# Cross attention in a two-layer kernel: value products split over the column halves of the PE array, softmax sums as separate 32-column products

## The reference, cut to what matters

```
q, k   = rmsnorm(per head) of layernorm(x) @ Wq.T, and of the two key projections
p      = exp(q @ k.T / 8 - max)                       # 1024 x 1101 per head and batch
o      = (p @ v) / sum(p)
x      = x + concat(o over heads) @ Wo.T + bo
```

## Time and profile before

| | before |
|---|---|
| median of 3 runs | 1112.41 us (1111.99 to 1117.14) |
| the profiled execution: its time | 1111.86 us |
| its span, from the first to the last instruction | 1110.1 us |
| TensorE busy in matmuls | 976.9 us, 88% |
| VectorE, ScalarE, GpSimd busy | 61%, 41%, 27% |
| granted TensorE clock, mean | 0.918 of full speed |

### The profile page before, as it was taken

One profiled execution on the slowest core, in us unless ns is written; L12 is line 12 of the kernel. 1 busy time (PEld: TensorE's weight loads), 2 busy tenths in 40 slices (PEclk: granted clock), 3 DMA queues, 4 the chain that ended last, 5 costly groups with the idle time before them and its releaser, 6 DMA issues.

```text
span 1110.1 us, 15593 instructions
## 1 busy us (share of the span) xinstructions
PE 976.9 (88%) x4575; PEld 667.7 (60%) x4576; DVE 678.1 (61%) x1355; ACT 453.1 (41%) x749; POOL 302.1 (27%) x249
## 2 busy tenths in 40 slices
PE   5796565695899999999999887999999999999992
PEld 3673333353555555555556665887777777777771
DVE  3277888477556456445638689755555555555555
ACT  2224888343355654565454431423222333223320
POOL 1000110123053455464452643001222222222210
PEclk9566888697699999999999998999999999999996
DMA  7300000000077577658675500019620178000304
GB/s 212 115 1 1 1 0 0 1 0 9 1 288 271 184 279 258 228 194 297 268 256 200 227 1 1 10 47 425 263 108 28 33 302 324 28 28 24 100 17 151
DMA packets 50180, 143.85 MB, mean 130 GB/s; under 512 B 7689, under 2 KB 26442, under 8 KB 45536
## 3 DMA queue, kind: packets, MB, share of 16 engines
q1 hardware_dynamic: 46400, 134.10, 32.4%
q0 software_dynamic: 3744, 9.31, 2.7%
HBM read 87.82 MB, written 56.49 MB: 130 GB/s over the span
## 4 chain that ended last, share of the span: by engine, by line
PE 76%; DVE 11%; ACT 7%; issue 3%; DMA 1%; SPq 0%; POOL 0%; DVEq 0%; ACTq 0%; POOLq 0%
PE banks L964 11%; PE banks L1185 7%; PE banks L1187 7%; PE banks L1186 6%; PE banks L884 4%; PE banks L936 3%; PE banks L1189 3%; PE banks L956 3%; PE banks L975 3%; PE banks L957 3%; PE banks L1055 2%; PE banks L1056 2%; PE banks L1057 2%; DVE small L1717 2%; PE banks L1204 2%
## 5 line engine op out<-in xcount | busy, mean ns | idle before, releaser
L964 PE MATMUL banks<-wexp 128*65 128x512 f32 (+1 forms) x288 | 148.2, 595 | 1.7 <-ACT wexp L1462 0.8
L1185 PE MATMUL banks<-ring,x_hi 128*128 x312 | 145.1, 465 | 0.8 <-issue 0.8
L1546 ACT ACTIVATE aux<-banks 128x512 f32<-128x512 f32 x78 | 46.7, 599 | 219.3 <-PE banks L1189 219.3
L561 POOL TENSOR_TENSOR cv_hl<-wexp,cv_hl 128x1024 fp32r<-128x1024 f32 x45 | 108.1, 2414 | 95.3 <-ACT cv_hl L1449 95.2
L1187 PE MATMUL banks<-ring,x_lo 128*128 x312 | 122.9, 394 | 0.0
L1186 PE MATMUL banks<-ring,x_hi 128*128 x312 | 122.3, 392 | 0.0
L1462 ACT ACTIVATE wexp<-banks 128x512 f32<-128x512 f32 x128 | 76.2, 601 | 112.9 <-PE banks L957 112.9
L1847 DVE TENSOR_REDUCE small<-banks 128x1 f32<-128x1101 f32 x64 | 83.5, 1304 | 46.8 <-PE banks L937 46.3
L956 PE MATMUL banks<-q_hi,k_hl 128*128 128x512 f32 x144 | 86.2, 598 | 0.7 <-ACT q_lo L1440 0.7
L2171 DVE TENSOR_TENSOR aux<-banks,aux 128x512 f32<-128x512 f32 x39 | 27.0, 691 | 79.7 <-ACT aux L1546 79.7
L936 PE MATMUL banks<-k_hl,q_hi 128*128 128x512 f32 (+1 forms) x192 | 66.3, 456 | 2.0 <-DVE k_hl L1842 2.0
(11 more groups left out here) (365 smaller groups left out, 2244.9 us busy)
## 6 DMA issues: line engine op xcount, KB each, us to landing
wsplit<-cv_hl SPq DMA_DIRECT2D x45, 1024.0 KB, 6.4
ring<-wsplit SPq DMA_DIRECT2D x32, 1280.0 KB, 12.0
wexp<-in_L_ffn_w SPq DMA_DIRECT2D x40, 512.0 KB, 4.4
ring<-wsplit SPq DMA_DIRECT2D x4, 1024.0 KB, 8.0
wexp<-moe_y SPq DMA_DIRECT2D x8, 512.0 KB, 6.7
wexp<-in_L_ffn_sw SPq DMA_DIRECT2D x5, 512.0 KB, 10.4
x_sb<-in_x SPq DMA_DIRECT2D x1, 2048.0 KB, 9.4
wexp<-in_L_ffn_W SPq DMA_DIRECT2D x2, 1024.0 KB, 7.2
```

The lines of the kernel that those rows point to most:

```text
L561: g.tensor_tensor(sides(hl[:, PIECE:2 * PIECE]), raw, sides(hl[:, 0:PIECE]).bitcast(f32), ALU.subtract).then_inc(s['cv_lo'], 1)
L964: mm(pb[5 + half][0:DA, :], vh[b][0:w, c, :], pT[q % 3][0:w, :], start=c == 0, stop=c == len(KTILES) - 1).then_inc(s['a_pv'], 1)
L1185: mm(o[:], x_hi[u][:, kc, :], hi, start=kc == 0, stop=False)
```

## The change

The value product of a key tile has 64 stationary columns instead of 65. That of the first half of the queries is placed in columns 0 to 63 of the array (rows 0 to 63 of bank 5), that of the second half in columns 64 to 127 (rows 64 to 127 of bank 6), and both are issued one behind the other, once per key tile: at odd q and at q = 17, behind the work on the neighbouring heads. The softmax sums are products of their own: 32 columns of ones against the same `pT`, for two key tiles and both halves together, each of the four in another quarter of the array's columns, into the other 64 rows of the same banks. So each bank holds 64 rows of values, and two times 32 rows of sums (even key tiles and odd key tiles). ScalarE copies 128 rows; the projection contracts over 128 rows with a weight that has ones in column 256 at one row of each of the two groups of sums and zeros elsewhere. As the two halves lie differently, the projection has two weights, `woT` and `wo_b`. `Wo` comes transposed from the host, so TensorE no longer turns it; `wo_b` is loaded by DMA and filled by GpSimd during head 0, and TensorE waits for both (`a_wo`, `ld_wo`) ahead of the loop over the heads. There are five `pT` buffers instead of three, given back by the sums, once per four units.

```
-        def values(n, b, q):
-            c, half = divmod(q, 2)
-            a, w = KTILES[c]
-            pe.wait_ge(s['a_p'], n * NU + (q + 1))
-            mm(pb[5 + half][0:DA, :], vh[b][0:w, c, :], pT[q % 3][0:w, :], start=c == 0,
-               stop=c == len(KTILES) - 1).then_inc(s['a_pv'], 1)
+        def values(n, b, c):
+            w = KTILES[c][1]
+            pe.wait_ge(s['a_p'], n * NU + (2 * c + 2))
+            for half in range(2):
+                mm(pb[5 + half][half * DH:(half + 1) * DH, :], vh[b][0:w, c, :], pT[P_AT[2 * c + half]][0:w, :], start=c == 0,
+                   stop=c == len(KTILES) - 1)
+
+        def sums(c):
+            for k in ((c - 1, c) if c % 2 else (c,)):
+                w = KTILES[k][1]
+                for half in range(2):
+                    row = (1 - half) * DH + k % 2 * 32
+                    last = mm(pb[5 + half][row:row + 32, :], ones[0:w, 0:32], pT[P_AT[2 * k + half]][0:w, :], start=k < 2,
+                              stop=k + 2 >= len(KTILES))
+            last.then_inc(s['a_pv'], 1)
...
-                mm(TP[:, 0:D + 1], oT[b][0:DA, t * P:(t + 1) * P], flat(woT[0:DA, bass.ds(h, 1), :]), start=True, stop=True)\
+                mm(TP[:, 0:D + 1], oT[b][:, t * P:(t + 1) * P], flat(wo[t * P // 512][:, bass.ds(h, 1), :]), start=True, stop=True)\
...
-                    if q == 0 and not first:
-                        pe.wait_ge(s['a_o'], n)
-                    values(n, b, q)
...
+                    if q == 1 and not first:
+                        pe.wait_ge(s['a_o'], n)
+                    if q % 2:
+                        c = q // 2
+                        values(n, b, c)
+                        if c % 2 or c == TB:
+                            sums(c)
...
+            pe.wait_ge(s['a_wo'], 1)
+            pe.wait_ge(s['ld_wo'], NLD['ld_wo'])
             with pe.Fori(0, NH - 1) as i:
...
-                    if q >= 3 or not first:
-                        act.wait_ge(s['a_pv'], n * NU + (q - 2))
+                    if q >= 5 or not first:
+                        act.wait_ge(s['a_pv'], n * PAIRS + used_before(q))
...
-                a(oT[b][0:DA, 0:512], pb[5][0:DA, :], ACT.Copy)
-                a(oT[b][0:DA, 512:S], pb[6][0:DA, :], ACT.Copy).then_inc(s['a_o'], 1)
+                a(oT[b][:, 0:512], pb[5], ACT.Copy)
+                a(oT[b][:, 512:S], pb[6], ACT.Copy).then_inc(s['a_o'], 1)
...
+            g.memset(wo_b[DH:P, :, D:D + 1], 0.0)
+            link(g.memset(wo_b[0:DH, :, :], 0.0))
+            for row in (0, 32):
+                link(g.memset(wo_b[row:row + 1, :, D:D + 1], 1.0))
+            pool.sem_inc(s['a_wo'], 1)
             for p in range(PER_STEP):
                 conv(p)
```

More of the change, by code:

```diff
@@ L13 @@
         'L1_ffn_sw3', 'L1_ffn_sb3', 'L1_ffn_sw2', 'L1_ffn_sb2']
+_TURNED = ('L1_xattn_Wo',)
 class Chain:
@@ L100, in program @@
         KW = -(-(S + SK) // 8) * 8
-        SPLIT = B * 4 * KW
+        SPLIT = B * 2 * (S + KW)
         HB_AT = (RING - 1) * WSP + 4400
@@ L118, in program @@
         hb = [(hb[2 * n], hb[2 * n + 1]) for n in (0, 1, 2, 7, 3, 4, 5, 6)]
-        _, *heads = aliased(("x_span1", XS + RING * WSP - SPLIT), *((f"{name}{u}", KW) for name in ("q_hi", "q_lo", "k_hl", "k_hi") for u in range(B)))
+        _, *heads = aliased(("x_span1", XS + RING * WSP - SPLIT), *((f"{name}{u}", S if name[0] == "q" else KW) for name in ("q_hi", "q_lo", "k_hl", "k_hi") for u in range(B)))
         q_hi, q_lo, k_hl, k_hi = (heads[n * B:(n + 1) * B] for n in range(4))
@@ L163, in program @@
         woT = scr.take(NH * (D + 1), NH)
-        scr.take(3 * SLOTS)
         mask_u = scr.take(SKB).bitcast(i32)
@@ L184, in program @@
         wkv_raw = scr.take(2 * KC * DC, 2 * KC)
-        wo_raw = scr.take(KC * D, KC)
         scr.at = first
@@ L188, in program @@
         k_dup = scr.take((TB + 1) * P, TB + 1)
-        vh = [scr.take((TB + 1) * DA, TB + 1) for _ in range(2)]
-        pT = [scr.take(512) for _ in range(3)]
+        vh = [scr.take((TB + 1) * DH, TB + 1) for _ in range(2)]
+        pT = [scr.take(512) for _ in range(4)]
         oT = [scr.take(S) for _ in range(2)]
@@ L202, in program @@
         p0 = ax.take(4 * SK, 4)
+        b2_all, bo1_all, gate_raw = ax.take(D), ax.take(D), ax.take(D)[0:E]
+        ax.at = NB
+        wo_b = ax.take(NH * (D + 1), NH)
+        pT.append(ax.take(512))
+        ax.at = AUX - B * 2 * D
         ckv = ax.take(B * 2 * D, B)
-        b2_all, bo1_all, gate_raw = ax.take(D), ax.take(D), ax.take(D)[0:E]
+        wo = [woT, wo_b]
         ax.at = 0
@@ L357, in program, with used_before @@
         CONV_END = (0, 2, 4)
+        P_AT = [q % 5 for q in range(2 * (TB + 1))]
+        PAIRS = (TB + 2) // 2
+        def used_before(q):
+            if q >= 5:
+                return (q - 5) // 4 + 1
+            prior = max(k for k in range(len(P_AT)) if P_AT[k] == q)
+            return prior // 4 + 1 - PAIRS
         PER_STEP = len(CONV_AT)
@@ L381, in _ @@
             load(wkv_raw[:], W['L1_xattn_Wkv'].rearrange("(t p) n -> p t n", p=P), 'ld_l1')
-            load(wo_raw[:], W['L1_xattn_Wo'].rearrange("(t p) n -> p t n", p=P), 'ld_l1')
+            load(woT[0:DH, :, 0:D], W['L1_xattn_Wo'].rearrange("(h d) n -> d h n", d=DH), 'ld_l1')
             for dst, w in ((lg, 'L1_xattn_ln_l_g'), (lb, 'L1_xattn_ln_l_b')):
@@ L428, in _ @@
                     load(bias_f[q, a:b], W[sn].rearrange("(a n) -> a n", a=1), 'ld_route')
+            sp.wait_ge(s['a_q'], 1)
+            load(wo_b[DH:P, :, 0:D], W['L1_xattn_Wo'].rearrange("(h d) n -> d h n", d=DH), 'ld_wo')
             for p in range(CONV):
@@ L518, in _ @@
             link(g.memset(ctxT[:], 0.0))
-            link(g.memset(woT[:], 0.0))
-            link(g.memset(woT[DH:DA, :, D:D + 1], 1.0))
+            g.memset(woT[0:DH, :, D:D + 1], 0.0)
+            link(g.memset(woT[DH:P, :, :], 0.0))
+            for row in (DH, DH + 32):
+                link(g.memset(woT[row:row + 1, :, D:D + 1], 1.0))
             g.iota(eno_i[:], pattern=[[0, 1]], base=0, channel_multiplier=1).then_inc(s['const'], 1)
@@ L564, in _ @@
             head(None, 0, 1)
+            pool.wait_ge(s['a_v'], 2)
+            pool.wait_ge(s['a_khi'], 2)
+            g.memset(wo_b[DH:P, :, D:D + 1], 0.0)
[3 more added lines that the diff above has]
+            pool.sem_inc(s['a_wo'], 1)
             for p in range(PER_STEP):
@@ L735, in turn_wkv @@
                 full(last)
-            def turn_wo(hp):
-                o = bank()
-                for j in range(2):
-                    h = hp * 2 + j
-                    for lc in range(KC):
-                        last = tr(o[0:DH, (j * KC + lc) * P:(j * KC + lc + 1) * P], wo_raw[:, lc, h * DH:(h + 1) * DH], ident[:])
-                full(last)
             def turn_gate():
@@ L771, in _ @@
             pieces = [[turn_wq, lambda: turn_wlkv(0), lambda: turn_wlkv(1), lambda: turn_wkv(0, P)],
-                      [lambda: turn_wkv(P, DC), weights_sums, lambda: turn_wo(0), lambda: turn_wo(1), turn_gate],
+                      [lambda: turn_wkv(P, DC), weights_sums, turn_gate],
                       [turn_ctx, lambda: turn_w1(0), lambda: turn_w1(1)],
@@ L1332, in _ @@
             pieces = [[keep_wq, lambda: keep_wlkv(0), lambda: keep_wlkv(1), lambda: keep_wkv(0, P)],
-                      [lambda: keep_wkv(1, DCR), lambda: keep_wo(0), lambda: keep_wo(1), keep_gate],
+                      [lambda: keep_wkv(1, DCR), keep_gate],
                       [keep_ctx, lambda: keep_w1(0), lambda: keep_w1(1)],
@@ L2233 @@
     for name in _INS:
-        a = np.ascontiguousarray(inputs[name])
+        a = inputs[name]
+        a = np.ascontiguousarray(np.transpose(a) if name in _TURNED else a)
         if a.dtype == np.bool_:
```

10 lines of the change are left out of this document (4 added, 6 removed).

## The result

The changed kernel takes 1135.32 us, the median of 4 runs (1134.66 to 1135.75); the kernel before, run beside it on the same chip, 1112.51 us (1111.99 to 1117.14, 4 runs). The ratio is 1.0205, with a 95% interval of 1.0177 to 1.0232: slower by 23 us. The profiled execution of after took 1135.42 us. I had forecast +95 us: the sign is right and the time lies in my range, but the size is wrong by four times. It came out near the rival "full overlap" (1131 us).

The account below looks back on a forecast made before the run. TensorE was taken to set the pace in the heads; heads 0 to 6 at +12.0 us each and head 7 at +10.7 gave +95 us on 1111.86, so 1207 us, range 1108 to 1245.

Parts of the forecast that it names:

- full overlap: Rival: both halves' first passes run together, 28 passes a head; +19 us, 1131 us, or 1113 with loads hidden; chance 0.22.
- What bounds the kernel: In the heads, TensorE alone sets the pace; what it gains or loses in a head moves the end one for one.
- Passes: Value and sum products in each head: overlap of one pass, 50 passes, 14 more than before, +6.0 us a head.
- The second half's late start: Products with new columns start late by their own exposed load, 0.06 or 0.03 us each: +0.9 us a head.
- Switches: Changes of the array's arrangement, 21 new a head at 0.09 us plus exposed loads: +3.35 us a head, head 7 3.75.
- The wait between the maxima: TensorE waits 0.57 us for VectorE's reading at three places in heads 0 to 6: +1.7 us each.
- The last head: Head 7, without the next head's maxima: +1.2 us under full overlap, 10.7 us in the main forecast.
- Costed at nothing: Turning of Wo, `wo_b` fill, SyncE's load waits, five `pT` buffers, 128-row copies and next head's first value product: no cost.
- The clock: Rival: a tenth of the heads' 395 us falls to the lower clock level, some 35 us more, 1242 us; chance 0.06.
- the likeliest case: Main forecast: overlap of one pass in program order, clock 1.00 in the heads; 1207 us, own range 1185 to 1225; chance 0.51.
- Faster: Rival: full overlap with switches under 0.09 us, loads included, makes the kernel faster; 1096 us with free switches; chance 0.07.

Follow-up runs that it names:

- e3: The changed kernel with both halves' value products in array columns 0 to 63 and the sums in 64 to 127, so halves cannot overlap: 1227.0 us (one run).
- e6: e5 with maxima and projection one unit later (q = 6 to 13) and the weight splitting's pieces moved to fit: 1113.51 us, ratio 1.0032.
- e5: The changed kernel with VectorE reading the maxima in two pieces, each bank part given back by itself: 1123.59 us, ratio 1.0117.
- e2: The kernel before, with its 65-column value products, but both halves issued at odd units as in the changed kernel: 1134.95 us, ratio 1.0216.
- e4: The changed kernel with four of the five groups of sums left out, so the softmax is divided by a wrong sum: 1109.81 us, ratio 0.9987.
- e9: e6 with each pair of value products at the even unit behind it and a sixth buffer for unit 17: 1118.07 us, ratio 1.0055.
- e1: The changed kernel with one more register operation on TensorE in the loop over the experts' tiles: 1135.3 us, ratio 1.0206.
- e10: e9 with the pair of q = 14 issued at q = 16: 1127.5 us, ratio 1.0142.
- e11: The order of e6 for heads 0 to 6 and that of e9 in head 7 alone: 1111.13 us, ratio 0.9994.
- e7: e6 with the value products of two key tiles together, four in a row at q = 3, 7, 11 and 15: 1118.79 us, ratio 1.0071.

## Why the prediction was right and wrong

**What bounds the kernel: right.** TensorE's own order set the end; each us it lost in a head came out one for one.

**Passes: the step that failed.** It reads "If TensorE starts matmuls in program order, the second half's first pass can start only when the first half's second pass has started. Then a pair takes 3 passes [...], a group of four sums 5." The trace shows both first passes together at 510.02 and 510.03 and both second ones at 510.50 and 510.51; e3 shows what it is worth. 28 passes and not 50: -3.4 us a head instead of +6.0. I had reasoned from rows in which every product used the same columns, and these cannot tell of products that don't. The Trainium skill, "TensorE: Matmul & The Clock Gate", Part 3, has strict program order with overlap between tiles: that the starts are in order the trace doesn't contradict (0.01 us apart), but I had taken a product's two passes to be neighbours in that order. How the passes of two products come to alternate, no run shows. The same page of the Trainium skill measures 2.38 times for three products of 32 columns, which by my estimate would have made four cost more than one; here four of two passes took 0.99 us, switch included, where one took 0.86. The Trainium skill, "TensorEngine Tiling (Array Packing)", Key Properties, says that tiles load and multiply independently and that a change of arrangement drains the engine; the trace agrees with both, the drain at 0.09 us.

**The second half's late start (+0.9): failed with it.** It is 0.01 us a pair.

**Switches (+3.35): right.** 0.09 and 0.11 on the way out, 0.09 and 0.06 on the way in for 64 columns and 0.12 from there to 32, as forecast from the one-column products. A head of e6 agrees: it is 0.15 us shorter than one of before, has 3.4 us of passes less and 0.2 us of waits more, so its switches come to 3.1 us.

**The wait between the maxima (0.57 us, three times): right**, by the rows of 513.79 and by e5, which takes it away and gains 1.45 us. Head 0, which I had counted like the others, costs 1.4 us in all.

**Nothing foreseen ahead of the first maxima: wrong, +1.2 us a head.** With a value product gone from in front of it, TensorE comes to the first maxima before ScalarE and VectorE have made `k_hl`. It appears in e2 too, grows in e4, and e6 removes it. The negated maxima wait a little too, 0.5 us a head.

So a head: -3.4 + 3.1 + 1.7 + 1.2 + 0.5 = +3.1, against 2.95 measured.

**The last head (+1.2 in the full-overlap rival): too small, measured +4.3.** Without the next head's work its values and projection wait for what the interleaved value products used to cover; in order of time of after:

```profile
585.24 1.08 PE L983 MATMUL banks<-wexp 128*64 128x512 f32 x4 [0.86 <-ACT wexp L1496]
588.20 0.70 PE L1004 MATMUL banks<-wexp 128*128 128x257 f32 x2 [0.32 <-DVE x_sb L1892]
```

The rows show a wait of 0.86 for an exponential and one of 0.32 for VectorE to give back the projection's bank. In the whole last head TensorE idles 1.9 us for exponentials and 1.2 for that bank, where it idled 0.8 before. e9, in which the values come later, takes 33.4 us, so the order can take back 0.7 of the 4.3.

**Costed at nothing:** in this trace nothing of the turning of Wo, of `wo_b` or of the buffers shows; the first value product of head 0 stands at 296.8 us, 296.4 before, 295.0 in e1.

**The rivals.** Full overlap gave 1131 us with a chance of 0.22, and e3 and the rows show it to be the mechanism; the 4 us missing are the first maxima (7), the negated maxima (3) and the last head (3), less what I had put for the late starts (7) and too much for head 0 (1) and the switches (1 to 2). Faster (0.07) would have wanted switches under 0.09 us; they cost about 0.15. The clock was 1.00 from 296 to 617 us, all through after's heads, as the likeliest case had it. The fear of a fall was not idle: e4, e6, e10 and e11 show single stretches at the lower level, 1.4 to 1.6 us each, where I had allowed for a tenth of the heads.

## What to carry to other kernels

Where products fill half or a quarter of the array's columns, count the passes that run together, then every change of arrangement with its drain and its exposed load: here 8 passes saved (3.4 us) and some 21 switches (3.1 us) cancelled. Fewer switches for each saved pass would be needed to win, and e7 shows that grouping for that brings its own waits. A product in the middle of an order is cover for other engines' work: moving it away cost some 20 of the 23 us here, and one kernel with the old products in the new order showed that at once. Look for what stands just behind the place that it leaves, all the way round the loop, and at the last turn, where no neighbour's work covers anything. And give the kernel before every edit that helps the new one before you call them equal: the best arrangement here is level with the kernel before, and 4.8 us behind it where both read the maxima in two pieces.

## What the hardware showed that I had not expected

Products of two passes in different column tiles run pass by pass: both first passes within 0.01 us, then both second ones. Four products of 32 columns took 0.99 us with their switch, where a single product of 65 columns holds the array for 0.86; put into the same columns two by two they took 1.85. And the granted clock can fall for a few us in the middle of a stretch that is 95% busy (e10, mean 0.97), right behind waits of TensorE of 0.6 to 1.6 us. Each such fall made its head 1.4 to 1.6 us longer: compare heads one by one, with their clock, before you put a difference down to the order of the products.
